# First slot of the second expert layer fixed to expert 0 and loaded ahead; scatter stages end without GpSimd's drain; router positions computed earlier

## The chip, the cores and the metric

The kernel runs on one core of a Trainium2 chip. The time is the device time of one execution in microseconds (us); several executions are timed, and their median is compared. The core has a matrix engine (PE; its weight loads are shown apart as PEld), a vector engine (DVE), a scalar engine (ACT), GpSimd (POOL) and SyncE (SP), which here issues most of the DMA transfers. Each engine follows its own list of instructions; they wait for each other through semaphores. A name with a q behind it (POOLq) is the engine's sequencer, which runs register, branch, drain, semaphore and DMA-issuing instructions.

## The reference

A decoder of two layers on x of 4 x 1024 tokens of width 256 (4096 tokens in all). Every step adds its result to x:

```python
x = x + L0_attn(ln(x), ...)                            # mamba: projection, conv, scan, projection
x = x + L0_xattn(ln(x), ctx, ctx, ctx)                 # gated product with the context's 77 rows
x = x + L0_ffn(ln(x), router_w, router_b, expert_w, expert_b)   # 8 experts, best one
x = x + L1_attn(ln(x), wq, wk, wv, wo)                 # causal self-attention, 16 heads
x = x + L1_xattn(ln(x), ctx, ctx, Wq, bq, Wk, ...)     # cross-attention, 16 heads
x = x + L1_ffn(ln(x), wg, bg, Wgate, Wup, Wdown)       # 8 experts, best two
```

The last step, which the change touches most:

```python
logits = xf @ wg.T + bg
vals, idx = jax.lax.top_k(logits, 2)
...
weights = jax.nn.softmax(masked, axis=-1)
for e in range(8):
    g = xf @ Wgate[e].T
    u = xf @ Wup[e].T
    h = g * jax.nn.sigmoid(g) * u
    out = out + h @ Wdown[e].T * weights[:, e:e + 1]
```

## The kernel before

The kernel is a sequence of stages, each written as one block with a program for each engine: constants (L168), mamba (L216), the context product with the first router (`_context_and_route`, L879 on), the first expert layer (`_expert_units`), the projections of self-attention (`_project_qkv`), self-attention itself, cross-attention with the second router (`_cross_attention`, L2208), and the second expert layer (`_expert_slots`, L2840). A block ends with a barrier: every engine drains, signals, and waits for the signal that all have come. At the end of a stage, and between the two halves of three of them, `K.clear()` (L91 to L94) then has POOL set the range of used semaphores to zero and runs a second barrier.

Two stages route. The 4096 tokens are taken in chunks of 4 tiles of 128 tokens; cross-attention has 8 chunks, 0 to 7. For each chunk DVE finds the best two experts of each token (`best_two`, `where`, `numbers`), marks them (`choose`), computes shares (`shares`); PE counts with triangular matrices how many tokens of each expert stand before each token (`places`); DVE makes of it the row numbers (`pick`, `slots_of`, `whole_slots`); and POOL writes each token's normalised row of 260 numbers into the DRAM tensor `t_h_sorted` at that row (`scatter`, L2562, 8 indirect DMAs a chunk). `t_h_sorted` has a region of 4096 rows for every expert, so that an expert's rows stand together. `normalise` (L2380) writes the normalised rows on DVE, `transposed`/`transposes` turn them on PE and ACT for the router's logits. The loop over n runs 32 tiles of attention and hangs the router's steps of older tiles on them: chunk c is normalised 9 steps behind and its places are computed 11 steps behind. At n=35 the two meet: `normalise(7)` and `choose(6)`.

After the last chunk DVE computes from the eight counts a table (`SlotTable`, L1406 on): `_expert_slots` runs 40 slots in a fixed order of sizes, and the table says for each slot which expert's weights it uses and at which row it begins. A slot is one expert's weights (gate, up, down: 3 transfers of 1 MB) and one or two units of 128 rows. SP loads, slot by slot, the slot's rows (`et_h`, L2889, after a read of the row number from the table, L2888) and then the next slot's weights (L2200, after a read of the expert's number, L2197); weights have three buffers. PE transposes the rows (`et_pT`, L2973), multiplies with gate and up (`et_pG`, `et_pU`, L2984) and down (`et_pO`, L2995); POOL adds the results to the output by indirect DMA (L2908), 71 of them.

Slot 0's weights are loaded at the end of cross-attention's block, behind the table, by these lines:

```python
            for ch in range(NCH):
                eng.wait_ge(s_res, (ch + 1) * TC)
                eng.dma_start(out[:, ch * TC:(ch + 1) * TC, :], R[:, ch * TC:(ch + 1) * TC, :]).then_inc(s_home, 16)
            eng.wait_ge(s_ready, 2)
            load_weights(eng, 0)
```

Of the kernel before, what the change touches and what calls it, by code (L numbers as in the profile page):

```python
# [38 lines left out]
TWOS, ONES = 31, 9  # L39
SLOTS = [1 if i % 4 == 3 and i < 4 * ONES else 2 for i in range(TWOS + ONES)]  # L40
# [3 lines left out]
assert sum(SLOTS) == 2 * TWOS + ONES and 2 * TWOS + ONES >= (TOP * TOK + 8 * (P - 1)) // P and ONES >= 8  # L44
# [834 lines left out]
def context_and_experts(K):  # L879

    with ExitStack() as c:
        table = {n: K.sb(c, f"t1_{n}", [P, len(SLOTS1)], d) for n, d in (("expert", I32), ("row", I32), ("expert_f", F32))}
        _context_and_route(K, table)
        K.clear()
        _expert_units(K, table)


def _context_and_route(K, table):
# [15 lines left out]
    with ExitStack() as c:  # L904
# [36 lines left out]
        block = c.enter_context(nc.Block())  # L941
# [331 lines left out]
def _expert_units(K, table):  # L1273
# [4 lines left out]
    with ExitStack() as c:  # L1278
# [16 lines left out]
        block = c.enter_context(nc.Block())  # L1295
# [110 lines left out]
class SlotTable:  # L1406


    def __init__(self, K, ctx, tag, twos, ones, ne):
        self.nc, self.twos, self.ones, self.ne, self.upto = K.nc, twos, ones, ne, twos + (ones + 1) // 2  # L1410
        sb = lambda n, shape: K.sb(ctx, f"{tag}_{n}", shape)
        self.number, self.unit, self.base, self.count = sb("number", [P, 64]), sb("unit", [P, ne]), sb("base", [P, ne]), sb("count", [P, ne])
# [13 lines left out]
    def prepare(self, eng):  # L1426
# [3 lines left out]
        for x in range(self.ne):  # L1430
            nc.vector.memset(self.base[:, x:x + 1], float(x * REGION))

    def pairs_and_ones(self, eng):
# [20 lines left out]
        nc.vector.tensor_scalar(jump2[:, :], twos[:, 0:NE], -2.0 * P, float(REGION), ALU.mult, ALU.add)  # L1454
        nc.vector.tensor_tensor(jump1[:, :], twos[:, 1:NE + 1], twos[:, 0:NE], ALU.subtract)
        ch.do(nc.vector.tensor_tensor_scan(end2[:, :], self.unit[:, :], twos[:, 0:NE], 0.0, ALU.mult, ALU.add))
        nc.vector.tensor_scalar(jump1[:, :], jump1[:, :], 2.0 * P, float(REGION), ALU.mult, ALU.add)
# [14 lines left out]
        ch.do(nc.vector.tensor_scalar(pair_row[:, :], pair_row[:, :], float(NE * REGION), None, ALU.min))  # L1472
        ch.do(nc.vector.tensor_reduce(one_row[:, :], moved[:, 0:ONES, :], axis=AX.X, op=ALU.add))
        ch.do(nc.vector.tensor_scalar(over[:, :], twos[:, 0:1], 2.0 * P, None, ALU.mult))
        ch.do(nc.vector.tensor_scalar(one_row[:, :], one_row[:, :], over[:, 0:1], None, ALU.add))
        nc.vector.tensor_copy(from_e[:, 0:ONES:2], pair_e[:, TWOS:UPTO])
        nc.vector.tensor_copy(from_e[:, 1:ONES:2], pair_e[:, TWOS:UPTO - 1])
        nc.vector.tensor_copy(from_row[:, 0:ONES:2], pair_row[:, TWOS:UPTO])
        ch.do(nc.vector.tensor_scalar(from_row[:, 1:ONES:2], pair_row[:, TWOS:UPTO - 1], float(P), None, ALU.add))
# [708 lines left out]
def cross_attention_and_experts(K):  # L2188

    with ExitStack() as c:  # L2190
# [3 lines left out]
        s_w = [c.enter_context(K.nc.semaphore(f"t2_w{q}")) for q in range(3)]  # L2194

        def load_weights(eng, i):
            e = eng.value_load(table["expert"][0:1, i:i + 1], min_val=0, max_val=K.io["t2_wgT"].shape[0] - 1)  # L2197
            for dst, name in zip(weights[i % 3], ("t2_wgT", "t2_wuT", "t2_wdT")):
                src = K.io[name][bass.ds(e, 1), :, :].rearrange("a (k p) n -> p (a k) n", p=P)
# [3 lines left out]
        K.clear()  # L2203
        _expert_slots(K, table, weights, s_w, load_weights)
    K.clear()


def _cross_attention(K, table, load_weights):  # L2208
# [23 lines left out]
    for n in range(DRAIN):  # L2232
        USES += [(f"T{g}", n - 2) for g in range(4)] * (2 <= n < NT + 2)
        for name, lag, count in (("LG", 10, 1), ("LN", -3, KD), ("Q", -2, KD), ("RT", 9, KD), ("PL", 11, 1)):
# [6 lines left out]
    with ExitStack() as c:  # L2241
# [33 lines left out]
        slots = SlotTable(K, c, "xs", TWOS, ONES, NE)  # L2275
# [11 lines left out]
        s_zero, s_bo, s_logit, s_ready, s_home = sem("zero"), sem("bos"), sem("logits"), sem("ready"), sem("home")  # L2287
# [3 lines left out]
        block = c.enter_context(nc.Block())  # L2291

        @block.sync
        def _(eng):
# [9 lines left out]
            eng.dma_start(router_b[:, :], io["t2_router_b"].partition_broadcast(P)).then_inc(s_in, 16)  # L2304
            out = io["out"].rearrange("b (t p) d -> p (b t) d", p=P)
# [3 lines left out]
            eng.wait_ge(s_ready, 2)  # L2309
            load_weights(eng, 0)  # L2310
# [4 lines left out]
        def _(eng):  # L2315
# [133 lines left out]
            slots.prepare(eng)  # L2449
            for x in range(NE):  # L2450
# [22 lines left out]
            for n in range(DRAIN):  # L2473
# [5 lines left out]
                ch = chunk_at(n, 9)  # L2479
                if ch is not None:  # L2480
# [591 lines left out]
```

## Time and profile before

| | |
|---|---|
| median of 3 runs | 3397.24 us (3391.85 to 3403.21) |
| profiled execution, its own time | 3387.4 us |
| its span in the profile | 3385.4 us |
| mean granted clock of PE | 0.940 |
| PE busy | 2950.8 us, 87% of the span |
| DVE, ACT, POOL busy | 61%, 42%, 45% |
| `_context_and_route` | about 1042 to 1165 us |
| `_expert_units` | about 1166 to 1246 us |
| `_cross_attention` | about 2251 to 2598 us |
| `_expert_slots` | about 2599 to 3385 us |

The profiled execution took 2.0 us more than its span; what lies outside the span is in no view. All positions in the text are microseconds from the span's start. A granted clock of 1.00 is 2.4 GHz, 0.50 is 1.2 GHz.

### The profile page before, as it was taken

To read this page: it belongs to the slowest core of one execution; us is meant where nothing else is said; L and a number is where in the kernel's file an instruction comes from. 1 tells how busy PE (TensorE), PEld (TensorE's weight loads), DVE (VectorE), ACT (ScalarE), POOL (GpSimd) and SP (SyncE) were. 2 spreads that over 40 slices of the span, in tenths; PEclk is the share of its full clock that TensorE was granted. 3 is DMA by queue.
4 is the path that set the end of the run, shared out by engine and by line. 5 is a ranking of instruction groups with operands and counts; after the bars stand their busy time and mean duration, and the time that the engine had idled before them with its cause. 6 is when DMAs were issued, how large, how long until landed. Compare 5 with 4: busy or idle time off the path is not lost. (4 is left out here: it accounts for less than half of the span.)

```text
span 3385.4 us, 43510 instructions
## 1 busy us (share of the span) xinstructions
PE 2950.8 (87%) x15258; PEld 1882.7 (56%) x15258; DVE 2062.4 (61%) x3871; ACT 1417.6 (42%) x2701; POOL 1508.7 (45%) x1189
## 2 busy tenths in 40 slices
PE   6998898899877679589989999979985999999998
PEld 2343343343334555355555555536664888888887
DVE  4998999899996546366666666648772222222221
ACT  5666767667642202145545545536551111111111
POOL 4787887788773540133233323236753111111111
PEclk8999999999998689699999999989896999999999
DMA  6135135225400261022222222210114565656662
GB/s 220 45 107 151 61 92 151 89 63 151 133 20 13 89 214 43 17 46 49 47 47 54 55 47 47 60 35 19 47 45 162 172 208 179 201 184 193 210 196 57
DMA packets 279943, 339.83 MB, mean 100 GB/s; under 512 B 84227, under 2 KB 236991, under 8 KB 279727
## 3 DMA queue, kind: packets, MB, share of 16 engines
q1 hardware_dynamic: 256479, 303.54, 29.9%
q0 software_dynamic: 16704, 27.21, 3.4%
q10 hardware_dynamic: 6544, 6.30, 0.6%
q8 instruction: 123, 2.02, 0.2%
q14 instruction: 93, 0.76, 0.1%
HBM read 231.55 MB, written 104.80 MB: 99 GB/s over the span
## 5 line engine op out<-in xcount | busy, mean ns | idle before, releaser
L489 POOL TENSOR_TENSOR mb_drive<-mb_dtx,mb_b_rep 128x1024 f32<-128x1024 f32 x256 | 598.9, 2357 | 182.9 <-DVE mb_pD L412 78.5
L791 PE MATMUL mb_pY<-mb_hc,ident 128*128 128x512 f32 x1024 | 506.0, 619 | 62.2 <-DVE mb_hc L423 61.8
L1759 DVE TENSOR_REDUCE at_nm_of<-at_pS 128x1 f32<-128x512 f32 (+3 forms) x768 | 408.0, 553 | 222.7 <-PE at_pS L1751 113.5
L1824 ACT ACTIVATE at_e<-at_pE 128x512 f32<-128x512 f32 x576 | 326.4, 598 | 347.8 <-PE at_pE L1815 345.7
L1831 POOL TENSOR_SCALAR_AFFINE_SELECT at_e<-at_e 128x256 f32<-128x256 f32 x256 | 156.4, 629 | 591.4 <-ACT at_e L1824 590.1
L2908 POOL DMA_INDIRECT out<-et_y,et_to x71 | 112.0, 1577 | 667.1 <-DVE et_y L2962 409.3
L2952 DVE TENSOR_TENSOR et_mT<-et_silu,et_pU 128x512 f32<-128x512 f32 (+1 forms) x160 | 100.2, 627 | 471.9 <-ACT et_silu L2923 471.9
L791 PEld LDWEIGHTS mb_pY<-mb_hc,ident 128*128 128x128 f32 x1024 | 191.5, 196 | 337.5 <-issue 182.1
L1747 PE MATMUL at_pS<-at_kT,at_qT 64*128 64x512 f32 (+3 forms) x768 | 301.6, 444 | 72.1 <-DVE at_nm_of L1759 67.3
L2923 ACT ACTIVATE et_silu<-et_pG 128x512 f32<-128x512 f32 (+1 forms) x160 | 87.8, 549 | 653.7 <-PE et_pU L2984 653.7
L537 ACT ACTIVATE mb_pD<-mb_dt,mb_a_neg 128x512 f32<-128x512 f32 x384 | 259.5, 688 | 156.5 <-DVE mb_hc L423 145.5
L406 DVE TENSOR_TENSOR_SCAN mb_pD<-mb_pD,mb_drive 128x1024 f32<-128x1024 f32 x128 | 292.8, 2287 | 43.3 <-ACT mb_pD L535 40.5
L412 DVE TENSOR_TENSOR_SCAN mb_pD<-mb_pD,mb_carried,mb_drive 128x512 f32<-128x512 f32 x256 | 313.9, 1269 | 7.2 <-ACT mb_pD L537 7.1
L423 DVE TENSOR_TENSOR mb_hc<-mb_pD,mb_c_rep 128x1024 f32<-128x1024 f32 x256 | 308.0, 1203 | 0.0
L2984 PE MATMUL et_pG<-et_hT,t_wg 128*128 128x256 f32 (+1 forms) x1280 | 274.2, 357 | 0.7 <-ACT et_hT L2918 0.7
L2984 PE MATMUL et_pU<-et_hT,t_wu 128*128 128x256 f32 (+1 forms) x1280 | 273.5, 357 | 0.0
L2995 PE MATMUL et_pO<-t_wd,et_mT 128*128 128x256 f32 x1136 | 268.2, 382 | 0.5 <-DVE et_mT L2952 0.5
L1812 PE MATMUL at_pE<-at_qT,at_kT 64*128 64x512 f32 (+3 forms) x768 | 240.5, 392 | 10.2 <-ACT at_e L1824 10.2
L1747 PEld LDWEIGHTS at_pS<-at_kT,at_qT 64*128 64x128 f32 x768 | 131.0, 188 | 205.1 <-DVE at_nm_of L1759 178.3
L2984 PEld LDWEIGHTS et_pG<-et_hT,t_wg 128*128 128x128 f32 x1280 | 226.6, 191 | 28.5 <-ACT et_hT L2918 1.1
L2984 PEld LDWEIGHTS et_pU<-et_hT,t_wu 128*128 128x128 f32 x1280 | 224.4, 191 | 26.1
L2995 PEld LDWEIGHTS et_pO<-t_wd,et_mT 128*128 128x128 f32 x1136 | 208.8, 190 | 25.6 <-DVE et_mT L2952 0.6
(452 smaller groups left out, 5042.5 us busy)
## 6 DMA issues: line engine op xcount, KB each, us to landing
t_wg<-in_t_wgT SPq DMA_DIRECT2D x40, 1024.0 KB
t_wu<-in_t_wuT SPq DMA_DIRECT2D x40, 1024.0 KB
t_wd<-in_t_wdT SPq DMA_DIRECT2D x40, 1024.0 KB
mb_b_rep<-mb_rows SPq DMA_DIRECT2D x64, 512.0 KB, 5.7
mb_c_rep<-mb_rows SPq DMA_DIRECT2D x64, 512.0 KB, 4.2
t_h_sorted<-blank SPq DMA_DIRECT2D x6, 4160.0 KB, 21.3
t_h_sorted<-blank SPq DMA_DIRECT2D x18, 1170.0 KB, 6.5
t_h_sorted<-blank SPq DMA_DIRECT2D x12, 1040.0 KB, 6.1
```

Of the source, the lines that this page charges most:

```text
L406: nc.vector.tensor_tensor_scan(both(pD), both(pD), both(drive), 0.0, ALU.mult, ALU.add).then_inc(s_scan, 2)
L412: nc.vector.tensor_tensor_scan(pD[r][:, k, :], pD[r][:, k, :], drive[r][:, k, :], carried[:, m, 2 * j + k:2 * j + k + 1], ALU.mult, ALU.ad ...
L423: nc.vector.tensor_tensor(hc[r][:, :, :], pD[r][:, :, :], c_rep[:, 2 * j:2 * j + 2, :], ALU.mult).then_inc(s_hc, 1)
L489: nc.gpsimd.tensor_tensor(drive[G % RINGS][:, :, :], dtx[:, m, :].unsqueeze(1).to_broadcast([P, 2, CH]), b_rep[:, 2 * j:2 * j + 2, :], ALU ...
L537: nc.scalar.activation(pD[r][:, k, :], dt[:, m, :], ACT.Exp, scale=scale).then_inc(s_dec, 1)
L791: last = nc.tensor.matmul(pY[:, :], K.ident[:, :], hc[G % RINGS][:, k, :], start=False, stop=(j == PAIRS - 1 and k == 1))
L1747: last = nc.tensor.matmul(pS[a][:, 0:w1 - w0], qT[b][side(a), h, qb * P:(qb + 1) * P], kT[b][side(a), h, w0:w1], start=True, stop=not diag)
L1759: nc.vector.tensor_reduce(nm_of[:, w0 // 512, a, qb:qb + 1], pS[a][:, 0:w1 - w0], axis=AX.X, op=ALU.max, negate=True).then_inc(s_max, 1)
L1812: nc.tensor.matmul(pE[a][:, at:at + w], kT[b][side(a), h, kb * P:(kb + 1) * P], qT[b][side(a), h, q0:q0 + w], start=(n == 0), stop=False, ...
L1824: nc.scalar.activation(e[g % NE][:, a, :], pE[a][:, :], ACT.Exp).then_inc(s_ex, 1)
L2984: last = nc.tensor.matmul(out[:, x, 0:w * P], weights[:, k, col:col + P], hT[q][:, k, 0:w * P], start=(k == 0), stop=(k == KD - 1))
L2995: last = nc.tensor.matmul(pO[q][:, a, :], mT[j][:, x, a * P:(a + 1) * P], wd[i % 3][:, j * PAIR + x, :], start=(j == 0 and x == 0 and a == ...
```

## The change

1. Four blocks, those of the two routing stages and of the two expert layers, are opened with `no_gpsimd_drain=True`. The other four engines still drain ahead of the block's closing semaphores, POOL does not.
2. `K.clear()` is called after mamba and after self-attention only. Five calls go between stages or halves of stages (after the constants, between router and experts of both layers, after the first expert layer), and two at the very end give way to one range clear on SP. (The semaphores of slot 0 to 2's weights are now in that range as well.)
3. The order of slot sizes is one unit, then eight times 2, 2, 2, 1, then seven times 2, instead of nine times 2, 2, 2, 1 and four times 2: 40 slots and 71 units in both. Slot 0 is fixed: expert 0, rows 0 to 127. Its weights are loaded by SP right behind the inputs of cross-attention, its rows need no read of the table, and the table starts expert 0 behind those rows.
4. Where one step of the loop has both, the places of the older chunk come ahead of the newer one's normalised rows (DVE) and transposes (PE, ACT).
5. Setting up the tables takes 18 more small DVE memsets; the rest of the table's code changes its operands, not its number of steps.

```diff
-TWOS, ONES = 31, 9
-SLOTS = [1 if i % 4 == 3 and i < 4 * ONES else 2 for i in range(TWOS + ONES)]
+TWOS, ONES = 31, 8
+SLOTS = [1] + [1 if i % 4 == 3 and i < 4 * ONES else 2 for i in range(TWOS + ONES)]
...
         _context_and_route(K, table)
-        K.clear()
         _expert_units(K, table)
...
-        block = c.enter_context(nc.Block())
+        block = c.enter_context(nc.Block(no_gpsimd_drain=True))
...
         for x in range(self.ne):
-            nc.vector.memset(self.base[:, x:x + 1], float(x * REGION))
+            skip = 0 if x else self.served
+            nc.vector.memset(self.base[:, x:x + 1], float(x * REGION + skip))
+            nc.vector.memset(self.region[:, x:x + 1], float(REGION - skip))
...
         def load_weights(eng, i):
-            e = eng.value_load(table["expert"][0:1, i:i + 1], min_val=0, max_val=K.io["t2_wgT"].shape[0] - 1)
+            e = eng.value_load(table["expert"][0:1, i:i + 1], min_val=0, max_val=K.io["t2_wgT"].shape[0] - 1) if i else 0
...
         _cross_attention(K, table, load_weights)
-        K.clear()
         _expert_slots(K, table, weights, s_w, load_weights)
-    K.clear()
...
             eng.dma_start(router_b[:, :], io["t2_router_b"].partition_broadcast(P)).then_inc(s_in, 16)
+            load_weights(eng, 0)
             out = io["out"].rearrange("b (t p) d -> p (b t) d", p=P)
             for ch in range(NCH):
                 eng.wait_ge(s_res, (ch + 1) * TC)
                 eng.dma_start(out[:, ch * TC:(ch + 1) * TC, :], R[:, ch * TC:(ch + 1) * TC, :]).then_inc(s_home, 16)
-            eng.wait_ge(s_ready, 2)
-            load_weights(eng, 0)
             eng.wait_ge(s_home, 16 * NCH)
...
-                ch = chunk_at(n, 9)
-                if ch is not None:
-                    normalise(ch)
                 ch = chunk_at(n, 11)
                 if ch is not None:
                     choose(ch)
...
                     whole_slots(ch)
+                ch = chunk_at(n, 9)
+                if ch is not None:
+                    normalise(ch)
...
-                r = eng.value_load(table["row"][0:1, i:i + 1], min_val=0, max_val=NE * REGION)
-                eng.dma_start(h[q][:, 0:w, :], K.h_sorted[bass.ds(r, w * P), :].rearrange("(a p) d -> p a d", p=P)).then_inc(s_h[q], 16)
+                rows = slice(0, w * P)
+                if i > 0:
+                    rows = bass.ds(eng.value_load(table["row"][0:1, i:i + 1], min_val=0, max_val=NE * REGION), w * P)
+                eng.dma_start(h[q][:, 0:w, :], K.h_sorted[rows, :].rearrange("(a p) d -> p a d", p=P)).then_inc(s_h[q], 16)
...
-STAGES = [load_and_constants, mamba, context_and_experts, self_attention, cross_attention_and_experts]
...
-        for stage in stages or STAGES:
-            stage(K)
-            K.clear()
+        load_and_constants(K)
+        mamba(K)
+        K.clear()
+        context_and_experts(K)
+        self_attention(K)
+        K.clear()
+        cross_attention_and_experts(K)
+        used = [x.num for x in K.in_use]
+        nc.sync.sem_clear(range(min(used), max(used) + 1))
```

SP's list, from the last input of cross-attention to the second slot's weights. The eight transfers `out<-resid` save the residual; the two branches are the end of one block and the start of the next; ISA rows are register work. Before:

```order
L2304 DMA xa_router_b<-in_t_router_b 128x8
L2308 DMA out<-resid 128x4x256 x8
L2197 TENSOR_LOAD t_expert
L2197 ISA x2
L2200 ISA
L2200 DMA t_wg<-in_t_wgT 128x2x1024
L2200 DMA t_wu<-in_t_wuT 128x2x1024
L2200 DMA t_wd<-in_t_wdT 128x8x256
L2241 UNCONDITIONAL_BRANCH
L2881 UNCONDITIONAL_BRANCH
L2888 TENSOR_LOAD t_row
L2889 DMA et_h<-t_h_sorted 128x2x260
```

and of the change:

```order
L2306 DMA xa_router_b<-in_t_router_b 128x8
L2204 DMA t_wg<-in_t_wgT 128x2x1024
L2204 DMA t_wu<-in_t_wuT 128x2x1024
L2204 DMA t_wd<-in_t_wdT 128x8x256
L2311 DMA out<-resid 128x4x256 x8
L2243 UNCONDITIONAL_BRANCH
L2884 UNCONDITIONAL_BRANCH
L2894 DMA et_h<-t_h_sorted 128x260
L2201 TENSOR_LOAD t_expert
```

Slot 0's three weight transfers have moved ahead of the eight that save the residual, both reads of the table ahead of slot 0 are gone, and its rows are one transfer of half the size.

DVE's list at n=35: chunk 7 is normalised (`xa_rows<-resid`), chunk 6 gets its row numbers. Before:

```order
L2399 TENSOR_TENSOR xa_behind<-xa_best 128x4
L2380 TENSOR_SCALAR xa_rows<-resid,xa_mv,xa_rstd 128x256 x4
L2403 TENSOR_TENSOR xa_chosen<-iota,xa_index_f 128x64
L2408 TENSOR_SCALAR xa_whole<-xa_expo 128x4
L2412 TENSOR_TENSOR xa_pairs<-xa_chosen 128x32
```

and of the change:

```order
L2429 TENSOR_TENSOR xa_sofar<-xa_sofar,xa_added 128x8
L2381 TENSOR_SCALAR xa_rows<-resid,xa_mv,xa_rstd 128x256 x4
L2433 TENSOR_TENSOR xa_picked<-xa_chosen,xa_place 128x64
L2438 TENSOR_REDUCE xa_slot_f<-xa_picked 128x8
L2444 CAST xa_slot<-xa_slot_f 128x8
```

The four normalising operations stand behind nine small ones that they stood ahead of, and still ahead of the last three that make the row numbers.

PE's list at the same step: `xa_pT<-ident,xa_rows` are chunk 7's transposes, the rows with `xa_pairs` and `xa_sofar` chunk 6's places. Before:

```order
L2741 MATMUL xa_pO<-xa_wo,xa_mixedT 128x256 x2
L2749 MATMUL xa_pT<-ident,xa_rows 128x128 x8
L2774 MATMUL xa_pT<-xa_pairs,xa_before 128x32
L2775 MATMUL xa_pT<-xa_sofar,xa_ones 128x32
L2777 MATMUL xa_pT<-xa_pairs,xa_ones 128x24
```

and of the change:

```order
L2744 MATMUL xa_pO<-xa_wo,xa_mixedT 128x256 x2
L2777 MATMUL xa_pT<-xa_pairs,xa_before 128x32
L2778 MATMUL xa_pT<-xa_sofar,xa_ones 128x32
L2780 MATMUL xa_pT<-xa_pairs,xa_ones 128x24
```

The places come ahead of the eight transposes.

## Rows read from the trace of the kernel before

**Rows 1.** Windows: stretch, length, busy us by engine, PE clock, DMA share, GB/s.
```profile
2615.00:3371.00 756.00, 753.83 (x3885) 668.67 (x3883) 170.89 (x573) 104.88 (x198) 108.88 (x69) 1.00 0.58 182
```

**Rows 2.** Chain that ended last, start of the slots: start us, us, what.
```profile
2598.79 0.27 SPq L2888
...
2599.54 6.00 DMA et_h<-t_h_sorted
...
2605.59 1.13 PE et_pT L2973 x4
...
2606.74 0.59 ACT et_hT L2918
...
2607.38 3.78 PE et_pG L2984 x8
```

**Rows 3.** End of router and first experts (L904, L1278): count, ns, first and last start.
```profile
L904 DVEq DRAIN  x1: 385/385/385, 1162.1 to 1162.1; - x1
...
L904 POOLq DRAIN  x1: 2678/2678/2678, 1162.4 to 1162.4; - x1
...
L1278 POOLq DRAIN  x1: 3240/3240/3240, 1243.0 to 1243.0; - x1
```

**Rows 4.** The range clears (L93) of the whole trace, same columns (ns min/median/max).
```profile
L93 POOLq EVENT_SEMAPHORE_RANGE_CLEAR  x7: 49/283/348, 5.0 to 3384.6; - x7
```

**Rows 5.** Cross-attention's start: its last input (L2304) and first matmul (L2783).
```profile
L2304 SPq DMA_DIRECT2D xa_router_b<-in_t_router_b x1: 433/433/433, 2257.2 to 2257.2; - x1
...
L2783 PE MATMUL xa_pS<-xa_ctxT,xa_wk x8: 707/721/881, 2260.7 to 2264.4; 128*128 128x308 f32 x8
```

**Rows 6.** Scatters (L2562), and around n=35 L2380 and L2443.
```profile
L2562 POOL DMA_INDIRECT t_h_sorted<-xa_rows,xa_slot x64: 956/960/1176, 2364.7 to 2589.8; - x64
...
L2380 DVE TENSOR_SCALAR xa_rows<-resid,xa_mv,xa_rstd x4: 406/406/408, 2563.9 to 2564.9; 128x256 f32<-128x256 f32 x4
...
L2443 DVE CAST xa_slot<-xa_slot_f x2: 171/181/191, 2570.3 to 2578.4; 128x8 uint32<-128x8 f32 x2
```

**Rows 7.** End of cross-attention's block (L2241).
```profile
L2241 DVEq DRAIN  x1: 1142/1142/1142, 2592.1 to 2592.1; - x1
...
L2241 POOLq DRAIN  x1: 5292/5292/5292, 2592.5 to 2592.5; - x1
...
L2241 DVEq EVENT_SEMAPHORE  x1: 21/21/21, 2597.9 to 2597.9; - x1
```

**Rows 8.** Windows (as rows 1): both tables' computation, and slot 0's start.
```profile
1153.10:1161.80 8.70, 0.00 (x0) 0.00 (x0) 7.83 (x48) 1.48 (x2) 5.90 (x6) 0.50 0.30 107
2578.50:2592.30 13.80, 0.00 (x0) 0.00 (x0) 8.66 (x49) 0.00 (x0) 9.51 (x10) 0.50 0.30 107
...
2605.50:2613.10 7.60, 6.84 (x18) 5.22 (x19) 0.96 (x8) 1.87 (x2) 0.00 (x0) 0.50 1.05 385
...
2597.00:2605.00 8.00, 0.00 (x0) 0.00 (x0) 0.00 (x0) 0.00 (x0) 0.43 (x3) 0.50 1.05 387
```

**Rows 9.** First rows of the first expert layer (tile `eu_h`, 1160 to 1173 us).
```profile
L1379 PE MATMUL eu_pT<-ident,eu_h x6: 421/421/477, 1169.9 to 1172.9; 128*128 128x128 f32 x6
...
L1308 SPq DMA_DIRECT2D eu_h<-t_h_sorted x4: 378/387/397, 1167.0 to 1170.9; - x4
```

**Rows 10.** The chain again: a later slot of one unit, gate to gate.
```profile
2674.15 0.89 PE et_pG L2984 x8
...
2685.29 1.73 PE et_pG L2984 x8
```

**Rows 11.** End of the last block: the chain's last scatter, and POOL's drain (L2848).
```profile
3376.82 1.55 POOL out L2908
...
L2848 POOLq DRAIN  x1: 3485/3485/3485, 3380.8 to 3380.8; - x1
```

**Rows 12.** End of self-attention's projections (L1503).
```profile
L1503 POOLq DRAIN  x1: 1120/1120/1120, 1335.6 to 1335.6; - x1
...
L1503 SPq COMPARE_BRANCH  x1: 41/41/41, 1367.3 to 1367.3; - x1
```

More of the change, by code:

```diff
@@ L43 @@
 assert sum(SLOTS1) >= (TOK + 8 * (P - 1)) // P
-assert sum(SLOTS) == 2 * TWOS + ONES and 2 * TWOS + ONES >= (TOP * TOK + 8 * (P - 1)) // P and ONES >= 8
+assert sum(SLOTS) == 1 + 2 * TWOS + ONES >= (TOP * TOK + 8 * (P - 1)) // P and ONES >= 8
 def after(eng, sem, i, per, k=None):
@@ L2193, in cross_attention_and_experts @@
         weights = [[K.sb(c, f"t2_{n}{q}", [P, rows, cols]) for n, rows, cols in (("wg", KD, HID), ("wu", KD, HID), ("wd", HID // P, D))] for q in range(3)]
[L2194 removed]
+        s_w = [K.sem(c, f"t2_w{q}") for q in range(3)]
         def load_weights(eng, i):
[L2197 removed]
+            e = eng.value_load(table["expert"][0:1, i:i + 1], min_val=0, max_val=K.io["t2_wgT"].shape[0] - 1) if i else 0
             for dst, name in zip(weights[i % 3], ("t2_wgT", "t2_wuT", "t2_wdT")):
[L2199 removed]
+                src = K.io[name][bass.ds(e, 1) if i else slice(0, 1), :, :].rearrange("a (k p) n -> p (a k) n", p=P)
                 eng.dma_start(dst[:, :, :], src).then_inc(s_w[i % 3], 16)
         _cross_attention(K, table, load_weights)
[L2203 removed]
         _expert_slots(K, table, weights, s_w, load_weights)
[L2205 removed]
 def _cross_attention(K, table, load_weights):
@@ L2274, in _cross_attention @@
         token = sb("token", [P, NT])
-        slots = SlotTable(K, c, "xs", TWOS, ONES, NE)
+        slots = SlotTable(K, c, "xs", TWOS, ONES, NE, served=P)
         row_f = sb("row_f", [P, len(SLOTS)])
@@ L2290, in _cross_attention @@
         heads = lambda T, m: T[:, m * HM:(m + 1) * HM]
-        block = c.enter_context(nc.Block())
+        block = c.enter_context(nc.Block(no_gpsimd_drain=True))
         @block.sync
@@ L2449, in _ @@
             slots.prepare(eng)
+            nc.vector.memset(table["expert_f"][:, 0:1], 0.0)
+            nc.vector.memset(row_f[:, 0:1], 0.0)
             for x in range(NE):
@@ L2687, in _ @@
                     mixed(n - 2)
+                ch = chunk_at(n, 11)
+                if ch is not None:
+                    places(ch)
                 ch = chunk_at(n, 9)
@@ L2827, in _ @@
                     product(n - 3)
+                ch = chunk_at(n, 11)
+                if ch is not None:
+                    places(ch)
                 ch = chunk_at(n, 9)
@@ L2831, in _ @@
                         transposes("RT", ch, k)
-                ch = chunk_at(n, 11)
-                if ch is not None:
-                    places(ch)
             out = turn("CN0", 0)
@@ L2878, in _expert_slots @@
             saved_by.append(written[i % 2])
-        block = c.enter_context(nc.Block())
+        block = c.enter_context(nc.Block(no_gpsimd_drain=True))
         @block.sync
```

36 lines of the change are left out of this document (18 added, 18 removed).

## The prediction

> **What bounds the kernel now.** I read the windows first: from 2615 to 3371 PE is busy for 753.83 of 756.00 us at clock 1.00 [rows 1]. So nothing inside the second expert layer can be gained by feeding PE better; a start that is earlier by x moves its end by x. Then I looked, in the chain of waits, at what stands ahead of that stretch: PE's first work there starts at 2605.59, behind 6.00 us of the transfer of slot 0's rows, behind SP's read of the row number at 2598.79 [rows 2]. From 2592.5 on POOL only drains [rows 7]. The other seams of the program show the same pattern, so the gain is a sum over seams, at which all engines wait, and not a matter of busy shares. About what a measurement of this kernel can tell from no change is 0.3%, 10.2 us.
>
> **Term 1: barriers without POOL's drain, first layer.** Router to experts: POOL's drain takes 2.68 us from 1162.4; DVE, the last of the others, has drained at 1162.1 + 0.385 = 1162.5 [rows 3]. Without POOL's drain the barrier waits for DVE and for POOL's arrival at 1162.4, so some 2.55 us go (2.68 less the 0.1 by which DVE is later). First experts to projections: the drain takes 3.24 us from 1243.0 [rows 3], no other engine comes after POOL there, and SP, ACT and PE start the next stage off that barrier: 3.3 us. Below: nothing at both, if the same work is only paid later (rival B). Above: all 5.9 us. I take 5.85, because POOL has already waited for its transfers by semaphore ahead of the drain, so that nothing that the next stage reads is still on its way.
>
> **Term 2: clears.** A clear takes 49 to 348 ns [rows 4] and a barrier behind it. At cross-attention's end the first barrier is left at 2597.9 [rows 7] and the second is past by 2598.79 [rows 2]: 0.8 us for the widest clear. I scale the rest by the clear's own length: 0.4 after the constants, 0.7 between router and experts, 0.6 after the first experts; together 1.7. Each delays all engines, so each counts in full; bounds, from the shortest and longest clear with 0.35 to 0.45 us around it: 1.2 to 2.4 us. What the clears do beside this, nothing in the trace waits for. The 0.8 of cross-attention's end is in term 3.
>
> **Term 3: cross-attention to slots.** Four edits meet here.
> (a) When the block can end. The scatters (median 0.96 us; 16 follow on the row numbers of chunk 6 at 2570.3, the last starting at 2589.8) [rows 6] make (2589.8 − 2570.75)/15 = 1.27 us from start to start, if I let the first start 0.45 us behind the row numbers' operation. The reordering takes the four normalising operations, 4 x 0.41 = 1.6 us [rows 6], from ahead of chunk 6's counting, and PE's eight transposes too. They are still ahead of the last three DVE steps, but run there while PE and ACT work, so I take 2 us off for chunk 6's numbers. Chunk 7's numbers, at 2578.4 [rows 6], depend on neither; the ninth scatter then starts at about 2578.9, 8 x 1.27 = 10.2 us behind the first at 2568.7. So the last starts at 2587.8, 2 us sooner. It no longer decides then: DVE ends its table at about 2592.3 with a drain of 1.14 us from 2592.1 [rows 7], thus at 2593.2 at the latest. Of its last 13.8 us it is busy for 8.66; the same computation in the first layer takes 8.70 us in all [rows 8]. If it waits as now, the barrier falls at 2593.3; if its waits hang on POOL's scatters or go, at 2590.5 (POOL has waited for the scatters' landing at 2592.5 [rows 7], less 2). I take 2592.5, nearer to the row as it stands, bounds 2590.5 and 2593.6.
> (b) No second barrier, no read of the row number. Instead of 2598.79, SP's program starts at 2592.55, and instead of at 2599.54 (0.75 us later [rows 2]) it issues the rows' transfer at once, at 2592.6.
> (c) The transfer of slot 0's rows now takes 6.00 us [rows 2], since 3 MB of weights are ahead of it at 387 GB/s from 2597 to 2605 [rows 8]. The nearest undisturbed row is the first experts' `eu_h`, of twice the size of the new one: issued at 1167.0, used at 1169.9, 2.9 us [rows 9]. Half the bytes cost less by 0.133 MB at 387 GB/s, 0.3 us: 2.6, bounds 2.3 and 2.9. PE starts at 2595.2, 10.4 us sooner than 2605.59.
> (d) One unit in slot 0: its two first transposes instead of four (1.13 us [rows 2]) save 0.6 us ahead of the first gate product; the work of the other units is all there later.
> Together 11.0 us. With the bounds of (a) and (c): 9.6 to 13.3.
>
> **Costed at nothing.** Slot 0's weights behind the inputs: they are issued behind the last input in SP's queue (2257.2, PE starts at 2260.7 [rows 5]), and nothing reads them for 330 us. Cover gone, if packets of the last inputs shared the engines with 3 MB, PE would start 8.1 us later at worst (3.15 MB at 387 GB/s [rows 8]). The saves of the residual behind them wait for data of much later. The 18 memsets, 8 in the first layer's routing and 10 in the second's: no row shows one so small; at 0.17 us each, like the smallest cast [rows 6], the ten take 1.7 us, beside the input transfers of their stage (3.5 us from the last issue to PE [rows 5]), and bare 1 to 2 us if that cover were full. Slot 1's weights: SP issues them behind slot 0's rows from about 2593.4, they need 8.1 us plus some 2, landing by 2604. Slot 0 needs PE for 11.14 us when warm [rows 10] and 2 to 3 more at clock 0.50, which now lasts to 2613.1, 7.6 us from PE's start [rows 8]: slot 1's gate product comes at 2595.2 + 1.2 + 14 = 2610, 6 us behind the landing. Slot 1's rows are behind those weights, by 2605.
>
> **Term 4: the end.** The last scatter starts at 3376.82, and POOL reaches its drain at 3380.8, which takes 3.49 us [rows 11], to 3384.3; then two clears with barriers fill up to 3385.4. Now the barrier falls at about 3380.9 and SP clears one range, at most 0.35 us [rows 4]: the end at 3381.3, 4.1 us sooner. Bounds: 0.6 (the drain's time is paid anyway) and 4.4.
>
> **The sum.** 5.85 + 1.7 + 11.0 + 4.1 = 22.65, say 22.7 us. Against the profiled execution, 3387.4 us (span 3385.4 and 2.0 outside it), that is 3364.7. The median of the runs shown is 9.8 us higher; I assume that the difference stays, thus 3374.5.
>
> **A rule against term 4.** The row shows the drain inside the span [rows 11]. The Trainium skill, "Runtime: NRT & Kernel Launch", section "The launch sequence", lists behind the kernel a barrier that waits for all engines (about 1.5 us) and a reset of the DMA rings (about 2 us). By it POOL's unfinished work could be waited for outside the span. No run here shows that yet; it is part of rival B.
>
> **Rivals.** A, the forecast, 0.55.
> B: the drain is no idle wait but work of POOL's own. For it speaks that it grows with the scatters: 2.68, 3.24 and 5.29 us behind 32, 39 and 64 of them, 0.083 us each [rows 3, 7], and 3.49 behind 71 [rows 11]. If the next POOL instruction, or the program's end, pays it, then the first experts' start loses what POOL's tables there hold up (2.6 of 5.85) and the end its 3.5; behind the projections POOL has 30 us in hand (1335.6 against 1367.3 [rows 12]), and at the slots it is needed only later. 22.7 − 6.1 = 16.6, median 3380.6; chance 0.14.
> C: a new wait at the slots: DVE's table sets the release at 2593.6, the rows queue behind something (6 us as now), or slot 1's weights come late by a few us. Each costs 1 to 4 us; gain 14 to 20, 3377 to 3383; chance 0.16.
> D, slower: slot 1's weights land so late that PE stands behind slot 0. It decides from the point at which the stall exceeds the other gains: they would have to land at 2610 + 22.7 + 10.2 = 2643, 49 us after issue, where 3 MB take 8 now. Only if the early weights also held up cross-attention's inputs (8.1 us) would less do. 3400 or more; chance 0.03.
> E: hardly any gain (under 10.2 us): POOL's drain is paid at every seam in another form, the clears are hidden and only term 3c is left (about 4 to 8 us), 3389 to 3393, or the runs' scatter (3391.85 to 3403.21) hides it; chance 0.12.
>
> A rule beside 3c: the Trainium skill, "DMA: Bandwidth & Descriptors", section "Anatomy of one DMA — SWDGE (gpsimd) path", fits 2.0 us plus bytes over 436e3. An estimate by it for 133 KB is 2.3 us, where I take 2.6 from [rows 9]; for that row's 266 KB it would be 2.6 against the 2.9 seen. By it the sum would be 0.3 us better.
>
> **Numbers.** A to C are faster by over 10.2 us: 0.85. E is same, 0.12; D slower, 0.03. A's own range is from its bounds: terms 5.85, 1.2 to 2.4, 9.6 to 13.3, 3.4 to 4.4, so 20 to 26 us, 3371 to 3377, and the run-to-run spread of 6 us around it. The range 3364 to 3388 leaves out D, most of E, and little else.
>
> **What would show it.** The spans between the closing semaphores and the drains at the three seams (no POOL drain, releases within 0.2 us of the last engine); POOL's first instruction behind each seam at once (A) or 2.6 to 5 us later (B); the chain at the slots with 2.6 us for the rows instead of 6.00; the first gate product near 2588.8 (2607.38 less 11.0 of term 3 and 7.55 of terms 1 and 2); PE with no wait at slot 1; last row some 4 us nearer to the last scatter. The prediction is wrong if PE waits for `t_wg` or `et_h` at slot 1, if cross-attention's first matmul comes later than 3.5 us behind the issue of the last input [rows 5], or if the time outside the span grows.

## The result and the profile after

The changed kernel takes 3359.99 us (median of four, 3358.93 to 3362.68) against 3397.76 us; the ratio is 0.9896 with a 95% interval from 0.988 to 0.9911, so 35 us faster (30 to 41). The forecast was 22.7 us faster, 3374.5 us, and its range began at 3364. The profiled execution took 3359.07 us, 1.6 us more than its span, where it was 2.0 before. Profiled against profiled the gain is 28.3 us, and by medians 37.8.

The chain of waits of the changed kernel at the start of the slots (start us, us, what), which answers to [rows 2]:

```profile
2582.18 2.04 DMA et_h<-t_h_sorted
2584.22 0.04 issue
2584.27 0.70 PE et_pT L2978 x2
2584.97 0.02 issue
2585.00 0.38 ACT et_hT L2923
2585.38 0.04 issue
2585.42 2.08 PE et_pG L2989 x8
2587.50 1.71 PE et_pU L2989 x8
```

The rows of slot 0 are in after 2.04 us instead of 6.00, the read of the row number is gone, and two transposes take the place of four. The gate products start at 2585.42, 22 us sooner; 2588.8 was forecast. The seams up to there make some 19 of the 22; the rest is stages between them that ran shorter in this execution.

The barriers, by line (count, ns min/median/max, first and last start), which answer to [rows 3, 7, 11, 12]. Router to experts:

```profile
L903 DVEq DRAIN  x1: 388/388/388, 1156.9 to 1156.9; - x1
...
L903 SPq EVENT_SEMAPHORE  x2: 17/17/17, 1038.6 to 1157.6; - x2
```

Cross-attention's end:

```profile
L2243 DVEq DRAIN  x1: 219/219/219, 2581.7 to 2581.7; - x1
...
L2243 POOLq COMPARE_BRANCH  x1: 43/43/43, 2581.1 to 2581.1; - x1
...
L2243 SPq EVENT_SEMAPHORE  x1: 17/17/17, 2582.1 to 2582.1; - x1
```

The program's end, and the end of self-attention's projections:

```profile
L2851 POOLq COMPARE_BRANCH  x1: 41/41/41, 3357.0 to 3357.0; - x1
...
L1507 POOLq DRAIN  x1: 6937/6937/6937, 1322.9 to 1322.9; - x1
...
L1507 SPq COMPARE_BRANCH  x1: 41/41/41, 1354.5 to 1354.5; - x1
```

No POOL drain stands at the four seams; each barrier is left within 0.6 us of the last engine's drain or POOL's arrival. At cross-attention's end the last is DVE, whose drain behind the table ends at 2581.9; POOL arrives at 2581.1. POOL's next full drain, in a block that kept it, is 6.94 us long where it was 1.12 [rows 12], and ends 25 us before SP gets there: some of the work was put off, to where nobody waits for it.

The windows view of the second expert layer (stretch, length, busy us of each engine, PE clock, DMA share, GB/s) answers to [rows 1]:

```profile
2590.00:3347.00 757.00, 756.23 (x3888) 671.18 (x3886) 171.42 (x574) 105.30 (x198) 108.84 (x69) 1.00 0.59 185
```

PE stands for less than 0.8 us from 2590 on, so slot 1 waits for nothing. What got worse is at cross-attention's start. The last input, and the clears (before: [rows 4, 5]):

```profile
L2306 SPq DMA_DIRECT2D xa_router_b<-in_t_router_b x1: 432/432/432, 2252.5 to 2252.5; - x1
...
DMA to landing us min/median/max: 4.7/4.7/4.7
...
L93 POOLq EVENT_SEMAPHORE_RANGE_CLEAR  x2: 312/504/697, 1035.3 to 2245.9; - x2
```

The input lands 4.7 us after its issue; before, PE had started 3.5 us after it. And the clear behind self-attention now takes 0.70 us, as its range of semaphores is wider.

To see whether the gain is at the seams, the places where all engines wait for one another, I measured each one between two fixed operations, in the three profiles of before (the one shown ahead, e1, e14) and the five of the changed kernel (the one above, e2, e8, e12, e13). Means in us, with the spread in brackets:

| from, to | before | changed | gain | forecast |
|---|---|---|---|---|
| router's table cast on DVE to first PE operation of the experts | 8.15 (8.07 to 8.27) | 5.05 (4.95 to 5.23) | 3.1 | 3.25 |
| last scatter of the experts to PE's first of the projections | 17.04 (16.78 to 17.20) | 13.07 (12.93 to 13.26) | 4.0 | 3.9 |
| issue of cross-attention's last input to PE's first there | 3.39 (3.18 to 3.52) | 4.86 (4.75 to 4.94) | −1.5 | 0 |
| chunk 7's row numbers to slot 0's gate product | 29.63 (28.96 to 30.38) | 16.71 (16.16 to 17.56) | 12.9 | 11.0 |
| start of the last down product to the end | 14.66 (14.60 to 14.70) | 10.57 (10.39 to 10.67) | 4.1 | 4.1 |

With 0.4 for the clear after the constants and −0.5 for the wider one the seams sum to 22.5 us. The forecast was 22.7, but that the sums agree is in part luck: the slots gave 1.9 us more than forecast, and cross-attention's start and the wider clear took back 2.0 that the forecast had at nothing. The question is where the other 5 to 13 us of the measured difference are. In the two profiles shown, 23 of the 28.3 us are at the seams, some 5 lie between them and 0.4 outside the span.

### The profile page after: what moved, and what is told of

It is laid out like the page before. It is cut to its first block and busy times, and to the rows that moved or that the text cites. A ratio compares the mean times of both kernels' runs of the same rounds, so it can differ in the third digit from the quotient of the medians.

```text
span 3357.5 us, 43453 instructions
## 1 busy us (share of the span) xinstructions
PE 2944.8 (88%) x15258; PEld 1880.4 (56%) x15258; DVE 2063.2 (61%) x3889; ACT 1418.0 (42%) x2701; POOL 1508.6 (45%) x1189
## 5 line engine op out<-in xcount | busy, mean ns | idle before, releaser
L3000 PEld LDWEIGHTS et_pO<-t_wd,et_mT 128*128 128x128 f32 x1136 | 209.0, 190 | 25.4 <-issue 0.6
```

Of the source, the lines that this page charges most:

```text
L3000: last = nc.tensor.matmul(pO[q][:, a, :], mT[j][:, x, a * P:(a + 1) * P], wd[i % 3][:, j * PAIR + x, :], start=(j == 0 and x == 0 and a == ...
```

## The experiments

Fourteen runs follow, of ten kernels: before (e1, e14), the changed one (e2, e8, e12, e13) and eight others. All timed comparisons are with before on the same chip. Seams are read from profiles, and of before there are only three: the one shown ahead, whose chip is not on record, and two from chip 10. None was taken on chip 7 with e5 to e8 or on chip 11 with e9 to e12. "At equal clock" is explained at e12.

**e1: before against itself.** No edit.

> The kernel before, unchanged, timed against itself. The median of before was 3397 us, its profiled execution 3387, and the changed kernel's gain was 37.8 us by medians but 27.9 us by the spans of the two profiled executions. Theory V (the stages that the change does not touch take a different time in each execution, mamba and self-attention by several us, and the profile of before caught a quick one): ratio 1.000 within 0.3%, and a profile whose mamba stage (1036.4 us from barrier to barrier before) or self-attention (883.2 us) differs by 3 us or more. Theory R (the change makes even those stages faster): the profile agrees with the first one in both stages within 1 us.

Ratio 0.9993 (0.997 to 1.0015). On that chip the 29 executions of before reach from 3381.56 to 3414.13 us, and this run's own 12 up to 3420.85. The windows of mamba and of self-attention, first of the profile shown ahead, then of this one:

```profile
4.90:1041.30 1036.40, 891.56 (x2064) 379.95 (x2064) 930.52 (x783) 666.80 (x1269) 797.20 (x416) 0.96 0.36 104
1367.60:2250.80 883.20, 775.89 (x5921) 455.33 (x5921) 537.58 (x1073) 426.55 (x800) 270.99 (x387) 0.96 0.21 46
```

```profile
5.00:1034.70 1029.70, 887.56 (x2064) 378.13 (x2064) 930.53 (x783) 667.40 (x1269) 797.92 (x416) 0.96 0.34 105
1365.50:2252.50 887.00, 778.39 (x5921) 456.69 (x5921) 538.03 (x1073) 426.70 (x800) 271.44 (x387) 0.95 0.19 46
```

The same program takes 6.7 us less in mamba and 3.8 more in self-attention. DVE, ACT and POOL are busy equally long; PE is busy for 4 us less and 2.5 more. Theory V holds: stages nobody touched differ by several us from one execution to the next.

**e2: the changed kernel again.** No edit.

> The changed kernel again. Its first profile had mamba at 1030.2 us and self-attention at 890.7 us between barriers. Theory V: both differ by several us from those, the gain is 33 to 38 us. Theory R: mamba again near 1030 and the same gain.

Ratio 0.9918 (0.9887 to 0.9949), median 3373.08 from six executions of 3358.71 to 3380.61. Mamba took 1032.4 us (1030.2 in the first profile), self-attention 890.6 (890.7). The forecast's 3374.5 would have been right on this chip. Theory V is met by half: mamba differs by 2 us, self-attention does not, and 28 us of gain came, below the 33 named.

**e3: drains alone.**

```diff
-        block = c.enter_context(nc.Block())
+        block = c.enter_context(nc.Block(no_gpsimd_drain=True))
```
(in the four blocks; clears kept)

> Before with the four blocks opened without GpSimd's drain, all clears kept. Theory A (the drain is an idle wait): 2.6 + 3.3 + 3.5 + 3.5 us at the four seams, some 13 us faster. Theory B (the drain is POOL's own work, paid by its next drain or instruction): the clear behind each seam has a drain of POOL's own (0.07 to 0.15 us before), which would then take 2.7, 3.2, 5.3 and 3.5 us, and the time stays within 2 us of before.

Ratio 0.9957 (0.9936 to 0.9979), 15 us. The clears' own drains on POOL and the next full drain, in this kernel:

```profile
L93 POOLq DRAIN  x7: 71/111/136, 4.8 to 3382.3; - x7
...
L1503 POOLq DRAIN  x1: 1111/1111/1111, 1332.4 to 1332.4; - x1
```

The drain in the clear does not grow, so theory B is out at these seams: the 2.7 to 5.3 us were not work that the next instruction must pay. Three seams gain 2.1, 3.4 and 3.4 us. Cross-attention's end gains nothing: from chunk 7's numbers to the gate product it is 30.8 us, 29.6 in the mean before. The end of the block (L2241) and the chain behind it show why:

```profile
L2241 POOLq COMPARE_BRANCH  x1: 38/38/38, 2588.0 to 2588.0; - x1
...
L2241 SPq DRAIN  x1: 7/7/7, 2593.3 to 2593.3; - x1
```

```profile
2595.11 7.84 DMA et_h<-t_h_sorted
```

POOL is there at 2588.0, but SP, which before came behind DVE's table with slot 0's weights and was hidden by POOL's drain, comes at 2593.3 and holds the barrier. And the rows, issued closer behind those weights, take 7.84 us, where the three profiles of before have 6.0 to 7.3. e10, on chip 11 and also without this drain, shows the same: 8.06 us for the rows and 31.7 us for the seam. On these two chips the removed drain pays here only if the weights have left this place too.

**e4: clears alone.** The seven clears removed as in the change, drains kept.

> Before with the clears removed as in the change, drains kept, one range clear on SP at the end. Both theories: 0.4 + 0.7 + 0.6 + 0.8 + 0.5 = 3 us faster by the seams. If instead the clears cost more than their barriers show (a hidden cost in the stage behind each), 5 to 15 us faster.

Ratio 0.9978 (0.996 to 0.9996), 7.5 us (1 to 14), which leaves both answers open. By the seams 0.8 and 0.9 us at the first layer's two, 0.4 after the constants, 0.5 at the end, −0.5 behind self-attention; at the slots the rows' transfer takes 7.42 us and the seam 29.6 us, as in the mean before. That is some 2 us, near the 3 expected; the 5 to 15 us of a hidden cost are not excluded by the time, but no seam shows them.

**e5: slot 0 alone**, with its early weights and its one unit.

> Before with slot 0 alone fixed to expert 0, one unit, its weights loaded behind the inputs; drains, clears and the loop's order as before. By the seams: the rows of slot 0 land in 2.0 to 2.1 us as in the two profiles of the changed kernel instead of 6.0 to 6.6 (4.2), no read of the row number (0.7), one unit (0.6), less 1.3 for the later first matmul of cross-attention: 4.2 us faster. If the seams' sum holds for the whole (theory S: 23 us of the change are all at its seams, the rest of the measured 28 to 38 is the spread of the clock from run to run), the time is 2 to 7 us below before. Theory H (something outside the seams gains too): over 8 us.

Ratio 0.9982 (0.9969 to 0.9995), 6.1 us. The rows take 2.07 us, and the last input lands 4.7 us after issue, also without the rest of the change:

```profile
2592.86 2.07 DMA et_h<-t_h_sorted
...
2594.97 0.70 PE et_pT L2981 x2
```

```profile
L2309 SPq DMA_DIRECT2D xa_router_b<-in_t_router_b x1: 432/432/432, 2264.9 to 2264.9; - x1
...
DMA to landing us min/median/max: 4.7/4.7/4.7
```

From chunk 7's row numbers to the gate product it is 23.8 us, 5.9 less than the mean before; less 1.4 at the start, 4.5 us. The time is within theory S's 2 to 7, but the seam is compared across chips, and e6 shows that this flatters it.

**e6: the order alone.** `normalise` behind `whole_slots`, `places` ahead of the transposes.

> Before with the order of places and normalising alone. Chunk 6's row numbers come 2 to 3 us sooner against chunk 7's (the two casts 8.1 us apart before, 11.0 after), the last scatter too, but POOL's drain is then behind DVE's table: theory S: 0 to 1 us faster. Theory H: the moved steps also speed up what follows them on PE, more than 3 us faster.

Ratio 0.9984 (0.9969 to 0.9999), 5.4 us: more than theory S allowed, and theory H's bound of 3 is met. The table runs from the last numbers of chunk 7 (second start of the first line) to the experts' numbers (second line), first in this kernel:

```profile
L2443 DVE CAST xa_slot<-xa_slot_f x2: 172/172/172, 2566.1 to 2577.1; 128x8 uint32<-128x8 f32 x2
...
L2527 DVE CAST t_expert<-t_expert_f x1: 185/185/185, 2586.5 to 2586.5; 128x40 int32<-128x40 f32 x1
```

then in e5, which has the old order and ran on the same chip:

```profile
L2447 DVE CAST xa_slot<-xa_slot_f x2: 172/182/191, 2564.2 to 2572.3; 128x8 uint32<-128x8 f32 x2
...
L2533 DVE CAST t_expert<-t_expert_f x1: 419/419/419, 2581.7 to 2581.7; 128x40 int32<-128x40 f32 x1
```

Slot 0's rows in e6, from the chain:

```profile
2596.80 3.43 DMA et_h<-t_h_sorted
2600.24 0.04 issue
2600.28 1.13 PE et_pT L2973 x4
```

The table takes 9.4 us in both, and 9.4 and 9.3 in e7 and e8: these are the four profiles from chip 7. In the twelve others it takes 12.3 to 17.2 us, in the three of before 13.7 to 16.0, with idle stretches of DVE that stand at other instructions in each profile. So on chip 7 the table is quick in either order; why, no run shows. SP issues slot 0's weights from the table, so in e6 their 3 MB are largely in when the rows are asked for, 9 us later instead of 5: 3.43 us instead of 6.0 to 7.3.

The order's own part is the barrier: POOL reaches the block's end 12.5 us behind chunk 7's numbers instead of 14.0 (14.1 in e5), and its drain ends 1.5 us sooner. The seam is 25.0 us here against 29.6 in the mean before, but most of these 4.6 us are the chip's. My estimate for before on chip 7 is 25.1 to 26.4 us: the 29.6, with 2.1 (e5) to 3.4 us (e6) for the rows in place of the mean of 6.6. By it the order is worth at most 1.5 us at this seam, and on chip 7 the gains there of e5 and of the whole change are 3 to 4.5 us smaller than against the mean before. Where the rest of the 5.4 us in time is, these runs do not show.

**e7: slot 0's weights later**, on top of the change.

```diff
-            load_weights(eng, 0)
...
+                if ch == 2:
+                    load_weights(eng, 0)
```

> The changed kernel with slot 0's weights issued behind the third save of the residual instead of directly behind the inputs. In the changed kernel the first matmul of cross-attention comes 4.75 and 4.82 us behind the issue of the last input, before 3.47 and 3.52. If the three weight transfers take bandwidth from the last inputs, it falls back to 3.5 us and the kernel is 1.3 us faster than the changed one; if the change's extra memsets or the wider clear are the cause, it stays at 4.8. Slot 0 must still start within 2.1 us of the issue of its rows.

The last input's landing:

```profile
L2306 SPq DMA_DIRECT2D xa_router_b<-in_t_router_b x1: 432/432/432, 2260.1 to 2260.1; - x1
...
DMA to landing us min/median/max: 3.3/3.3/3.3
```

PE starts 3.3 us behind the issue: the cause was the three weight transfers, not the memsets or the clear. Slot 0's rows still take 2.11 us. In time the two kernels can't be told apart (3362.20 us, ratio 0.9939, against 3361.91 us, 0.9936, on the same chip); 1.5 us is below what six executions show.

**e8: the changed kernel, second chip.** No edit.

> The changed kernel once more, for the size of its gain: theory S gives 23 us, ratio 0.993 with an interval from 0.991 to 0.995; theory H 30 us or more, 0.991 or less. At the seams the same as in the two profiles so far, within 0.3 us: 5.0 us from the table's cast to the first matmul of the first experts, 12.9 from the last scatter to PE's first of the projections, 16.2 from chunk 7's row numbers to the first gate product, 10.5 from the last down product to the end. The whole span differs by several us with the granted clock.

Ratio 0.9936 (0.9913 to 0.996), 21.6 us. This chip runs before in 3381.86 us, where the chip of e1 needed 3398.84: two chips differ by 17 us in the same program, about as much as the change is worth. One stage stands out: from cross-attention's first PE operation to chunk 7's row numbers the four profiles from chip 7 take 302 to 305 us, the twelve others 312 to 321. All four seams named are within 0.3 us. At the slots, though, it is POOL's arrival that releases the barrier here (2585.6, where DVE has drained at 2582.6).

**e9 and e10: one drain back, at the end.** The last block is opened with the drain; e9 on the changed kernel, e10 on e3.

> The changed kernel with GpSimd's drain back in the last block alone. Before, that drain took 3.48 us behind its 71 scatters. In the changed kernel the drain of the projections' block took 6.94 us, against 1.12 before, behind the 32 + 39 scatters of two blocks without a drain and without a clear between them. Theory K (POOL keeps a debt for each scatter until its next full drain): the drain now covers 64 + 71 scatters and takes 3.5 + 5.3 = 8.8 us, or 13 at 0.098 us each, and the end is later by that. Theory L (the debt ends by itself with the time that passes): 3.5 us. Either way the loss against the changed kernel is the drain's length.

> Before with three blocks without GpSimd's drain, the last with it, all clears kept. In the run without any of the four drains and with the clears, the drain of the projections' block took 1.11 us, as before: a clear in between seems to end the debt for nothing. Theory K with that: 3.5 us here, for the 71 scatters since the last clear. If the clear has no part in it: 9 us or more.

The drains, of e9 and then of e10:

```profile
L2851 POOLq DRAIN  x1: 4439/4439/4439, 3379.1 to 3379.1; - x1
```

```profile
L2848 POOLq DRAIN  x1: 3489/3489/3489, 3385.5 to 3385.5; - x1
```

e10 is as theory K with the clear has it, and as L; it is a single execution, read for its drain alone. e9 is neither: 4.44 us, 1 us more than the 3.48 before, where K wanted 8.8 or more. So a debt that sums up over scatters fits the projections' drain (6.94 us, where 1.12 and the two left out make 7.04) but not the end, and what makes the one drain 4.44 us stays open. The end stood 15.1 us behind the last down product, 4.5 later than in the changed kernel; the timed ratio, 0.9888 (0.9873 to 0.9903), doesn't show that loss.

**e11: all four drains back**, on the changed kernel.

> The changed kernel with the drain back in all four blocks, clears gone. By the seams it loses against the changed kernel 2.6 (router to experts), 3.3 (experts to projections), about 5.3 (cross-attention to slots; the rows of slot 0 still land in 2.1 us) and 3.5 us (the end): 14.7 us, leaving about 8 us against before. If the drain's time can be hidden behind the rest of a seam, it loses under 8.

The seams lose 2.5, 3.7, 4.8 and 3.5 us against the changed kernel, 14.5 together, as expected (at the slots 4.2 against e12 on the same chip). The projections' full drain is 1.12 us again, as in e4: it grows only where drains and clears are both left out. The ratio is 0.9917 (0.9904 to 0.9931), 28 us faster than before on that chip, 6 us slower than e12. The plain times are thus off the seams' sum again, by 20 us on this chip, and the clocks differ: 0.9426 in the mean of these five executions, 0.9369 in the nine of before.

**e12: the changed kernel, third chip.** No edit.

> The changed kernel for the last time, for the size of its gain. On two chips it was 27.9 us (17 to 38) and 21.6 us (13 to 29), at its first measurement 35.3. Seams alone give 23. Theory S: 18 to 29 us, ratio 0.992 to 0.995; theory H: 30 or more.

Ratio 0.99 (0.9885 to 0.9916), 34 us: theory S's range is missed, theory H's met. Each execution comes with its mean granted clock, though, and I fitted time against it, over all executions with a level for each chip and each kernel. The fit with e13 and e14 in it (189 executions):

```
slope: -2312 +- 95 us per 1.00 of mean clock (-2.3 us per 0.001), rest 3.2 us
kernel against before at equal clock, us:
changed -19.7 +- 0.8   all drains back -12.0 +- 1.8   drains alone  -9.5 +- 1.0
clears alone -5.1 +- 1.0   slot 0 alone -6.5 +- 1.1   order alone -4.4 +- 1.1
changed, weights later -17.0 +- 1.5   changed, last drain back -21.0 +- 1.8
means, before and changed: us, clock
chip 7   3382.2 0.9382 (23)   3361.4 0.9397 (6)
chip 10  3397.8 0.9379 (70)   3370.5 0.9410 (12)
chip 11  3402.7 0.9369 (9)    3368.8 0.9423 (4)
```

Gains of 21, 27 and 34 us go with clocks that are higher by 0.0015, 0.0031 and 0.0054. Idle stretches cut out raise the mean by themselves: 22.5 us at 0.50 instead of 0.94, over 3390 us, by 0.0029. What goes beyond that, 0.0025 on chip 11, is worth 5.8 us.

**e13 and e14: a test of that line**, with both kernels on one chip.

> The changed kernel on whatever chip comes next. Over the 154 executions so far a straight line through time against mean granted clock, with a level for each chip and each kernel, has a slope of 2374 us per 1.00 of clock (2.4 us per 0.001) and leaves 3.3 us; at equal clock the changed kernel is 18.9 us below before. Theory S: again 19 us (16 to 22) at equal clock, and the plain difference of the medians is 19 us plus 2.4 us for every 0.001 by which the changed kernel's mean clock is higher. The rise by the shorter idle stretches alone is 0.0026 (23 us at 0.50 instead of 0.94, over 3400 us), so 25 us if the clock draws are alike. Theory H (a gain outside the seams that has nothing to do with the clock): at equal clock over 24 us.

> The kernel before again on the same chip, for the executions at its own clocks. Ratio 1.000 within 0.2%, and its times on the same line against the clock: 2.4 us for each 0.001.

e13: ratio 0.9917 (0.9893 to 0.9942), 28 us. e14: 1.0 (0.9985 to 1.0016). A line through both kernels' executions there (6, and all 29 of before) gives 21.5 ± 1.5 us at equal clock and 2.2 us for 0.001; the means differ by 27.8 us and the clocks by 0.0028. That lies in theory S's 16 to 22; H's 24 is less than two errors away and not excluded. And S took its range from the earlier fit: it says that the gain at equal clock repeats, not that all of it is at the seams.

## Why the prediction was right in its parts and wrong in its number

**The range and the median.** The step that failed is "The median of the runs shown is 9.8 us higher; I assume that the difference stays", with "the run-to-run spread of 6 us around it". The miss against 3374.5 is 14.5 us. Of it 8.9 are this step: the changed kernel's median lay 0.9 us above its profiled execution, not 9.8. The other 5.6 are the profiled difference of 28.3 against 22.7, nearly all of it between the seams and outside the span. e1 and e8 show why neither number could carry it: executions of before reach over 39 us on one chip (3381.56 to 3420.85), and chips differ by 17 in the median. The trace told where to look, since the clock is 0.73 to 0.96 in the stages before the slots and 1.00 only in the slots, but three executions of before were no measure of the spread.

**Terms 1 and 2** hold: 3.1 and 4.0 us at the two seams where 3.25 and 3.9 were forecast. Missed is that clears left out make the next one wider (0.70 us, 0.5 us lost).

**Term 3** was forecast at 11.0 and measured at 12.9 us, 0.7 of it because before's mean is 29.6 us where its first profile has 28.96. The release came 12.8 to 14.2 us behind chunk 7's numbers (14.1 forecast). As forecast, DVE's table decides it in four of the five profiles, 0.7 to 2.0 us behind POOL's arrival; on chip 7 (e8) POOL's arrival behind the last scatter does, 3.0 us behind DVE. The 1.14 us of DVE's drain [rows 7] that went into it was of that one profile: it is 0.22 in the two others of before and in the changed kernel. The rows took 2.0 to 2.2 us, under my 2.6 and under its lower bound of 2.3. The Trainium skill, "DMA: Bandwidth & Descriptors", section "Anatomy of one DMA — SWDGE (gpsimd) path", gave an estimate of 2.3 us for them, by a fit made for the GpSimd path, which was nearer than my row. One unit saved 0.6 us as said.

**Costed at nothing:** slot 1's weights and the memsets rightly, slot 0's weights not. They cost 1.5 us of waiting at cross-attention's start, between my 0 and the worst case of 8.1; e7 shows that they are the cause and that a later place avoids it. The prediction named this as a sign of being wrong, a first matmul later than 3.5 us behind the last input's issue, and it came: 4.75 us.

**Term 4** holds: 4.1 us. The time outside the span went from 2.0 to 1.6 us, so the barrier and ring reset that the Trainium skill, "Runtime: NRT & Kernel Launch", section "The launch sequence", lists behind a kernel took over nothing of it.

**Rivals.** B is out: no seam pays (e3), though a drain further on is longer, free only because 25 us of cover lie behind it. C came in one form, the weights' contention, at cross-attention's start; at the slots DVE's table does set the release, as C has it, but at 12.8 to 14.2 us behind chunk 7's numbers and not at 15.2. D and E did not come. The parts don't add: at equal clock the four alone make 25.4 us and the whole 19.7. Part of this may be that e5 and e6, both from chip 7, gain some 3 to 5 us more than their seams by the estimate at e6, which no run explains; against that, e3 misses a gain, since SP's issue of slot 0's weights holds the barrier that POOL no longer does.

**What stays open.** At equal clock the seams' 22.5 us should show as 15.8 us: cutting them raises the mean clock by 0.0029 by itself, and the line takes 2.3 us off for each 0.001. 19.7 ± 0.8 were seen. So some 4 us are neither in the seams nor in the line. A few us are more than the line can resolve, though: it puts e9, which by its seam should come 3.2 us behind the changed kernel (4.5 less the 0.3 of each that the mean clock takes back), 1.3 ahead of it, and e7, which should be ahead, 2.7 behind. The profiles show no gain between the seams: there the three of before have 3315.8 us in the mean (3312.9 to 3317.8) and the five of the changed kernel 3316.0 (3308.1 to 3325.1), and the spans differ by 22.5 us, the seams' sum. One piece that the seams leave out is small: the clock stays at 0.50 for 5.6 to 7.6 us past PE's start in the slots before and for 4.0 to 5.8 us in the changed kernel, in the mean 1.7 us less at half speed, worth 0.9. The gain of 35 us in the first four executions I take as seams plus a quick draw: their clock is 0.943 in the mean, where twelve executions on chip 10 have 0.941, and the line makes that 4.6 us. What made the draw quick no run shows.

## What to carry to other kernels

A seam at which all engines wait is worth its full length, and three of the five were priced to 0.2 us from the trace; the two at which transfers share the DMA engines were off by 1.5 and 1.9. A semaphore wait for the scatters made POOL's drain at a block's end spare here. Before an earlier issue is credited, look at what is then directly ahead of it in the same queue: here the drain's 5 us at the last seam were worth nothing until 3 MB of weights had left SP's list there. And a forecast of the total needs the spread of executions and of chips, with the clock beside each time; where it is as large as the change, compare seam by seam, and only profiles from the same chip: e6's seam looked 4.6 us shorter than before's, and at most 1.5 were the edit's.

## What the runs showed of the hardware

- Two chips run the same program in 3381.9 and 3398.8 us (medians of 23 and 29 executions), and executions of it on one chip lie up to 39 us apart; 2.3 us go with each 0.001 of mean granted clock, over 189 executions.
- The same computation on DVE, the table ahead of the slots, takes 9.3 to 9.4 us in all four profiles from one chip and 12.3 to 17.2 us in the twelve others, whatever the kernel.
- POOL's drain at a block's end takes 2.68, 3.24, 5.29 and 3.48 us behind 32, 39, 64 and 71 scatters, also when all transfers have been waited for. Left out, its cost comes back neither in the next POOL instruction nor in the small drain of a clear (0.11 us), yet a later full drain took 6.94 us instead of 1.12 when no clear lay between (1.11 and 1.12 where clears or drains alone were left out, e4, e3 and e11), and 4.44 instead of 3.48 at the end.
- 3 MB issued behind the last small input let it land after 4.7 instead of 3.3 us, though it was issued first.
